# Moving a split and the end of a sum between GpSimd, VectorE and TensorE in a pipelined two-layer kernel

## What is computed

```
x = layernorm(x + attention_0(x))      # 16 heads of 8, softmax with a distance bias
x = layernorm(x + experts_0(x))        # 8 experts, top 2, silu(x W1) * (x W3) W2, and a shared one
x = layernorm(x + attention_1(x))      # each token looks at shifted copies of k and v
x = layernorm(x + experts_1(x))        # 8 linear experts, top 2
```

```
for i, off in enumerate(OFFSETS):
    if off >= N: continue
    vs = v if off == 0 else shift(v, off)
    out = out + attn[..., i:i+1] * vs
gate = sigmoid(x @ w_gate + b_gate)
return gathered * gate @ w_out + b_out
```

## Time and profile before

| | |
|---|---|
| median of 3 runs | 1559.63 us (1558.98 to 1560.1) |
| profiled execution, own time | 1561.28 us |
| its span, first to last instruction | 1559.5 us |
| TensorE busy | 1392.1 us, 89% of the span |
| VectorE busy | 1319.1 us, 85% |
| ScalarE busy | 843.3 us, 54% |
| GpSimd busy | 660.3 us, 42% |
| mean granted TensorE clock | 0.97 |
| chain that ended last | VectorE 39%, TensorE 38%, issue 10%, DMA and ScalarE 4% each |

### The profile page before, as it was taken

One profiled execution on the slowest core, in us unless ns is written; L12 is line 12 of the kernel. 1 busy time (PEld: TensorE's weight loads), 2 busy tenths in 40 slices (PEclk: granted clock), 3 DMA queues, 4 the chain that ended last, 5 costly groups with the idle time before them and its releaser, 6 DMA issues.

```text
span 1559.5 us, 34559 instructions
## 1 busy us (share of the span) xinstructions
PE 1392.1 (89%) x11872; PEld 1081.4 (69%) x11872; DVE 1319.1 (85%) x4159; ACT 843.3 (54%) x1806; POOL 660.3 (42%) x484
## 2 busy tenths in 40 slices
...
DMA packets 77931, 145.90 MB, mean 94 GB/s; under 512 B 8747, under 2 KB 64299, under 8 KB 64683
## 3 DMA queue, kind: packets, MB, share of 16 engines
...
## 4 chain that ended last, share of the span: by engine, by line
DVE 39%; PE 38%; issue 10%; DMA 4%; ACT 4%; POOL 1%; DVEq 0%; ACTq 0%; POOLq 0%; SPq 0%
DVE prod L917 8%; PE bPV L495 7%; DVE nBy L974 7%; PE bTU L479 6%; DVE mneg L1021 5%; DVE h L1031 5%; DVE nDy L955 5%; PE bS L538 4%; DMA prod<-d_w 3%; PE bTU L481 3%; PE bTU L550 2%; PE b L419 2%; PE bTU L551 2%; PE bS L541 2%; PE b L436 2%
## 5 line engine op out<-in xcount | busy, mean ns | idle before, releaser
L1085 POOL TENSOR_TENSOR prod<-prod 128x1024 f32<-128x1024 f32 (+2 forms) x160 | 290.0, 1813 | 205.7 <-DVE prod L917 198.1
L1093 POOL TENSOR_TENSOR prod<-kC,qC 128x512 f32<-128x512 f32 x256 | 322.3, 1295 | 125.7 <-ACT kC L672 125.7
L1021 DVE TENSOR_REDUCE mneg<-bS 128x2 bf16<-128x512 f32 x512 | 346.5, 693 | 32.8 <-PE bS L541 32.7
L708 ACT ACTIVATE sil<-bTU,b 128x256 f32<-128x256 f32 x288 | 136.7, 475 | 306.0 <-PE bTU L551 302.9
L698 ACT ACTIVATE P<-bTU 128x512 f32<-128x512 f32 x512 | 279.3, 603 | 11.8 <-PE bTU L481 11.4
L538 PE MATMUL bS<-stack 96*128 96x256 bf16 x1024 | 222.7, 279 | 52.3 <-DVE mneg L1021 46.1
L479 PE MATMUL bTU<-stack 97*128 97x256 bf16 x1024 | 209.8, 276 | 0.4 <-DMA stack<-mT 0.2
L541 PE MATMUL bS<-dist,identh 128*128 128x128 f16 x1024 | 198.9, 222 | 0.0
L917 DVE TENSOR_TENSOR prod<-prod,vC 128x512 f32<-128x512 f32 x256 | 185.0, 776 | 15.1 <-DMA prod<-d_w 15.1
L481 PE MATMUL bTU<-dist,identh 128*128 128x128 f16 x1024 | 192.0, 221 | 0.0
L550 PE MATMUL bTU<-x1T,w 128*128 128x256 f32 x576 | 175.9, 387 | 6.0 <-DVE h L1031 6.0
...
## 6 DMA issues: line engine op xcount, KB each, us to landing
...
```

Of the source, the lines that this page charges most:

```text
L1021: v.tensor_reduce(mneg[:, :, k], bS[k % 2][:].rearrange("p (a b) -> p a b", a=TT), op=ALU.max, axis=AX.X, negate=True).then_inc(dveS.done( ...
L1085: tt_(pv[e % 2][:, to:to + rows_, :], pv[e % 2][:, to:to + rows_, :], pv[e % 2][:, frm:frm + rows_, :], ALU.add).then_inc(poolSum.done("ad ...
L1093: tt_(prod[e % 2][:, 2 * p:2 * p + 2, :], shifted(kC, p), qC[:].unsqueeze(1).to_broadcast([128, 2, T]), ALU.mult).then_inc(poolC1.done("pr ...
```

## The change

Three things are changed.

First, GpSimd stops its sum over the 16 rows at four: C2.add.3 and C2.add.4 are gone. A new step on TensorE, C2.sm, adds the four rows with four fp32 matmuls against the identity into a bank of the bTU round (now 34 steps instead of 33), and C2.gt reads this bank. Second, A1.rest and A1.lo are done by GpSimd, and its wait for the constants moves to the pass in which A3 starts. Third, the order of the steps is new on all engines.

```
     "pool": """
-        A3.xbo C2.xb C1.prod.0 C1.prod.1 C1.prod.2 C1.prod.3 C1.prod.4 C1.prod.5 C1.prod.6 C1.prod.7 C2.add.0
-        C2.add.1 C2.add.2 C2.add.3 C2.add.4""",
+        A1.rest A1.lo C1.prod.0 C1.prod.1 C1.prod.2 C1.prod.3 C1.prod.4 C1.prod.5 C2.add.0 C1.prod.6 C1.prod.7
+        C2.add.1 C2.add.2 A3.xbo C2.xb""",
     "sp": """
-        A3.x Cs.dw A1.part.0 Cs.wb A1.part.1 C2.wb X.xT A1.part.2 A1.rows.0 A1.rows.1 A1.rows.2 M.m D2.out""",
+        A1.part.0 X.xT A1.part.1 Cs.dw Cs.wb C2.wb A3.x A1.part.2 A1.rows.0 A1.rows.1 A1.rows.2 M.m D2.out""",
...
+                    if what == "C2.sm" and (e := r["C2"]) is not None:
+                        take(turn_bank("sm", 0), ("C2", dveC2, "gt", 0), t)
+                        o = bTU[turn_bank("sm", 0)]
+                        pe.wait_ge(poolSum.sem, poolSum.count(e, "add", 2))
+                        for x in range(4):
+                            i = mm(o[:, 0:T], ident[:], pv[e % 2][:, x, :], start=(x == 0), stop=(x == 3))
+                        i.then_inc(peC2.done("sm"), 1)
...
-                        dve.wait_ge(poolSum.sem, poolSum.count(e, "add", 4))
+                        dve.wait_ge(peC2.sem, peC2.count(e, "sm"))
                         dve.wait_ge(actV.sem, actV.count(e, "g"))
                         dve.wait_ge(peC2.sem, peC2.count(e - 1, "out"))
-                        v.scalar_tensor_tensor(gat[:], tg[e % 2][:], 1.0, pv[e % 2][:, 0, :], ALU.add,
+                        v.scalar_tensor_tensor(gat[:], tg[e % 2][:], 1.0, bTU[turn_bank("sm", 0)][:, 0:T], ALU.add,
...
+                    if what == "A1.rest" and (e := r["A1"]) is not None:
+                        pool.wait_ge(actA1.sem, actA1.count(e, "hi", 1))
+                        tt_(rest[:], qk[:], parts[:, :, 0, :], ALU.subtract).then_inc(poolA1.done("rest"), 1)
+                    if what == "A1.lo" and (e := r["A1"]) is not None:
+                        pool.wait_ge(st_part[2], dma_count(e - 1))
+                        pool.wait_ge(actMid.sem, actMid.count(e, "mid"))
+                        tt_(parts[:, :, 2, :], rest[:], parts[:, :, 1, :], ALU.subtract).then_inc(poolA1.done("lo"), 1)
...
-                        to, frm, rows_ = ((0, 4, 4), (8, 12, 4), (0, 8, 4), (0, 2, 2), (0, 1, 1))[n]
+                        to, frm, rows_ = ((0, 4, 4), (8, 12, 4), (0, 8, 4))[n]
```

More of the change, by code:

```diff
@@ L49 @@
     "pe": """
[L50 to L54, removed]
+        A1.qk A1.v S.s.0 A2.ST.0 S.s.1 Cs.scT A2.ST.1 A2.ST.2 A2.ST.3 S.s.2 A2.ST.4 A2.ST.5 A2.ST.6 A2.PV.0 A2.ST.7
@@ L55 @@
+        A2.ST.8 S.s.3 A2.ST.9 A2.PV.1 B.xT A2.ST.10 S.s.4 D.xT A2.ST.11 Cs.wT S.s.5 B.lg S.s.6 D.lg C1.xT A2.ST.12
+        A2.ST.13 C1.qk A2.ST.14 A2.PV.2 A2.ST.15 S.s.7 S.s.8 B.cT D.y.0 B.ab.0 A2.PV.3 S.s.9 D.y.1 B.ab.1 S.s.10
+        A3.pT B.ab.2 B.ab.3 C1.vg B.ab.4 S.s.11 S.s.12 D.y.2 B.y.0 B.ab.5 B.ab.6 B.ab.7 S.s.13 C1.sc A3.aT B.y.1
+        B.ab.8 S.s.14 S.s.15 D.y.3 A3.out B.y.2 B.y.3 M.mT C2.sm B.z C2.out""",
     "act": """
-        A1.qk A2.exp.0 A2.exp.1 A2.exp.2 A2.exp.3 A2.exp.4 A2.exp.5 A3n.nm A2.exp.6 C2n.nm B.xT Cs.exp D.xT A2.exp.7
@@ L57 @@
-        A2.exp.8 B2.nm A2.exp.9 A1.mid Cs.wT A2.exp.10 C1.xT G.ge A2.exp.11 A2.exp.12 C1.qk A2.exp.13 A2.exp.14 B.cT
-        A2.exp.15 D2.nm B.ab.0 B.ab.1 A3.cp B.ab.2 C1.vg B.ab.3 B.ab.4 B.ab.5 A3.aT C1.sc B.ab.6 B.ab.7 B.ab.8 M.mT""",
+        A1.qk A2.exp.0 A2.exp.1 A2.exp.2 A2.exp.3 A2.exp.4 Cs.exp A2.exp.5 A2.exp.6 A2.exp.7 A2.exp.8 A3n.nm C2n.nm
+        B.xT A1.mid B2.nm D.xT Cs.wT A2.exp.9 A2.exp.10 C1.xT A2.exp.11 A2.exp.12 G.ge D2.nm C1.qk A2.exp.13
+        A2.exp.14 A2.exp.15 B.cT B.ab.0 A3.cp B.ab.1 B.ab.2 B.ab.3 C1.vg B.ab.4 B.ab.5 B.ab.6 B.ab.7 A3.aT B.ab.8
@@ L59 @@
+        C1.sc M.mT""",
     "dve": """
[L60 to L63, removed]
@@ L64 @@
-        B.acc.2 C2.gt B.acc.3 C2.res""",
+        B2.res A1.v S.max.0 D2.mom Cs.mx N.root.0 N.root.1 S.max.1 N.root.2 N.root.3 S.max.2 Cs.sum S.max.3 S.max.4
+        S.max.5 S.max.6 G.rank G.weigh S.max.7 S.max.8 D.acc.0 S.max.9 B.wu.0 D.acc.1 S.max.10 B.wu.1 C2.pv.0
+        C2.pv.1 C2.pv.2 C2.pv.3 B.wu.2 A3.rec B.wu.3 B.wu.4 S.max.11 D.acc.2 B.acc.0 A3.num B.wu.5 C2.pv.4 C2.pv.5
+        C2.pv.6 C2.pv.7 B.wu.6 S.max.12 S.max.13 B.wu.7 B.acc.1 B.wu.8 S.max.14 S.max.15 D.acc.3 B.acc.2 A3.res
+        C2.gt B.acc.3 C2.res""",
@@ L224, in network @@
         actG = steps("actG", "ge")
-        dveA1, dveS = steps("dveA1", "rest v lo"), steps("dveS", "max*16")
+        dveA1, poolA1, dveS = steps("dveA1", "v"), steps("poolA1", "rest lo"), steps("dveS", "max*16")
         dveA3 = steps("dveA3", "rec num*2 " + LN)
@@ L657, in one @@
                         act.wait_ge(st_part[1], dma_count(e - 1))
[L658 removed]
+                        act.wait_ge(poolA1.sem, poolA1.count(e, "rest"))
                         nc.scalar.copy(parts[:, :, 1, :], rest[:]).then_inc(actMid.done("mid"), 1)
@@ L893, in one @@
                 for what, n in ORDER["dve"]:
-                    if what == "A1.rest" and (e := r["A1"]) is not None:
-                        dve.wait_ge(actA1.sem, actA1.count(e, "hi", 1))
-                        v.tensor_tensor(rest[:], qk[:], parts[:, :, 0, :], ALU.subtract).then_inc(dveA1.done("rest"), 1)
                     if what == "A1.v" and (e := r["A1"]) is not None:
```

19 lines of the change are left out of this document (7 added, 12 removed).

## The result

The changed kernel takes 1551.49 us (median of 5 runs, 1548.16 to 1552.75) against 1559.63 before: ratio 0.9944, 95% interval 0.9933 to 0.9955. It is faster by 0.56%; I had predicted 1577 us, slower by 1.1%, and had given "faster" two chances in ten. The time lies inside the range, the sign is wrong. The profiled execution, on which the readings rest, took 1548.16 us (span 1546.4), against 1561.28 (span 1559.5) before: 13.1 us less in the pair of profiled executions, 8.1 between the medians (the profiled execution after is the fastest of its five runs).

A forecast was written before the change was run, and what follows sets the result against it. TensorE alone bounds: 43.18 us own work, 1.32 wait at the head and 0.45 small waits make 44.95 us a pass, 0.67 more. 27 passes add 18 us, start and drain 0: 1579 profiled, 1577 median; range 1545 to 1600.

The forecast's parts named there:

- TensorE's own work: TensorE's time in a pass without waits: 41.35 us before, plus 1.83 for C2.sm and a switch, 43.18 us.
- drain and start: Last passes without score work, and program start: -1 us and +1 us, sum 0, between -7 and +7.
- the fixed head: A2.ST.3 starts 4.78 us after A1.qk, held by ScalarE's table load and exp.0; TensorE waits 1.32 us; chance 0.48.
- wait of VectorE for xout: Sign in the changed kernel's trace: nDy was not to wait for xout.
- The small waits: TensorE waits at A2.ST.6, B.xT, D.xT and B.lg, together 0.45 us a pass.
- Edits costed at nothing: Two subtractions, A1.rest and A1.lo, moved from VectorE to GpSimd: no cost, except 1 us at program start.
- the two adds off GpSimd: Adds of 1.27 and 0.73 us removed from GpSimd: worth nothing in a full pass, as C2.gt does not wait there.
- The port between VectorE and GpSimd: VectorE's products beside GpSimd's: charged nothing; by the skill's lockout rule up to 0.8 us more a pass.
- The early Cs.mx: Cs.mx before the root in the drain: gives its chain to wb 1.5 to 2 us in three passes.
- (b): All TensorE waits go or part of its counted work was waiting: 43.18 us a pass, 1530, half 1545; chance 0.20.
- (d): Small waits and extra switch vanish, only A2.ST.3's wait stays: 44.40 us a pass, drain -3, 1560; chance 0.14.
- (c): C2.add.2 to C2.out uncovered by B.z, or B.acc.0 holds B.ab.7: 0.5 to 1.5 us a pass, 1590 to 1617; chance 0.18.

The follow-up runs named there:

- e12: Changed kernel with D.y.3 moved between S.s.14 and S.s.15 on TensorE, one more change between bf16 and fp32 matmuls; 1552.14 us.
- e3: Changed kernel with A1.rest and A1.lo back on VectorE; 1551.35 us.
- e4: Kernel before with only A1.rest and A1.lo moved to GpSimd; 1559.05 us.
- e2: Changed kernel without C2.sm, all five adds on GpSimd, the new order and the moved subtractions kept; 1571.54 us.
- e6: Changed kernel without C2.sm, five adds on GpSimd, A3.xbo and C2.xb ahead of C2.add.1, C2.gt ahead of A3.res on VectorE; 1557.03 us.
- e1: Kernel before with only C2.sm added on TensorE and three adds instead of five on GpSimd; 1596.59 us.
- e5: Changed kernel without C2.sm, five adds on GpSimd, A3.xbo and C2.xb moved ahead of C2.add.1; 1545.51 us.
- e7: Changed kernel with one matmul in C2.sm instead of four, rows 1 to 3 left out of the sum; 1524.20 us.
- e15: Changed kernel with Cs.mx behind N.root and Cs.exp behind exp.6 only in passes behind the last with S steps; 1555.42 us.

## Why the prediction was wrong

The bound was named rightly; two terms of the sum were mis-sized. TensorE's own work was put at 43.18 us a pass and measured 42.76, and drain and start were put at nothing and measured -11.3 us in the profiled pair. The first term alone takes the forecast from slower to no change: a pass of 44.33 us is nearly the 44.28 of before. It is the second that makes the kernel faster, and that gain was not foretold.

**TensorE alone as the bound, with the fixed head: right.** 81% of the chain, 4.78 us from A1.qk to A2.ST.3, 1.27 us of waits in it against 1.32. No wait of VectorE for xout, VectorE busy for 39.2 us, C2.sm 1.83 with its change of kind: all as foretold.

**TensorE's own work: mis-sized.** I had 43.18 us. Waits in the changed pass are 1.27 at the head and about 0.3 behind it, so the own work is 44.33 - 1.57 = 42.76. C2.sm is as summed; the rest fell from 41.35 to 40.93, by moving alone. About 0.3 of it lies in the gaps at changes of kind. Their number is 16 in each direction in both orders, but B.y.0, which stood directly behind S.s.15 and carried 0.14 us, now follows D.y.2, D.xT carries 0.06 instead of 0.11, and the 0.10 us that the first matmul of B.y.3 carried behind M.mT now falls on C2.sm, within its 1.83. I took such gaps as fixed; e12 shows them as 0.07 us and movable. Some 0.1 us is not accounted for.

**The small waits: nearly right.** 0.45 forecast, 0.3 found: B.xT and B.lg wait as laid out, A2.ST.6 only 0.10, D.xT not at all. With the own work as found, the pass is 44.33 and not 44.95: 0.62 x 27 = 17 us of the 31 by which the sum (1579) missed the profiled execution; the odd passes are 3 more.

**Edits costed at nothing: right for the subtractions** (e3, e4). **Wrong for the two adds off GpSimd, "worth nothing" in a full pass.** I judged them by the old order, where C2.gt didn't wait for GpSimd. In the new order A3.xbo stands behind the adds, and with all five there the pass is 44.75 at least and the total 20 us longer (e2). Of a step that is taken off a queue, what stands behind it on that queue in the new order counts too.

**The port between VectorE and GpSimd: charged nothing, rightly.** GpSimd's prod.5 ends 0.3 us before C2.pv.0 starts, and C2.pv.0 took 0.68 to 0.69 us in each of the 27 passes. So the 0.8 us a pass of the rule cited there was not put to the test in the changed kernel; e6 did so (last section).

**Drain and start: -1 and +1 forecast, -8.5 and -2.8 found**, the other 11 us. Of the three passes for which I charged C2.sm at half clock (3.5 us) only the last had it (3.75 us; the one before it 1.96), and in e1 the whole sum costs the drain 6.7 us, in the new order nothing that shows against the two adds that it replaces (216.9 against 217.6 in e5). Its matmuls are not free there: with three of the four left out the drain is 212.1 (e7). The early Cs.mx is worth up to 5 us, as I had put it (1.5 to 2 in three passes), but about half of that comes by another way, the wait at A2.PV.1 (e15). What was missing is the wait of 2.26 us at B.xT with the halved clock behind it. I read the earlier trace rows from late in the drain, where TensorE idles anyway, and took no rows of its first pass, where it is busy for 39 of 44 us and the order counts as in a full pass.

At the start, the first interval between two S.max.0 fell from 19.2 us to 16.7. It was 16.9 in e4 (subtractions moved alone) and 17.4 in e3 (subtractions back), and stayed 19.2 in e1. I had charged 1 us where some 2 were won. The subtractions alone win them, and the rest of the change wins them without the subtractions, so the two don't add up. The interval varies: in e15, which is the changed kernel there, it was 17.3.

**The rivals.** None came as written. (b) named the right cause, "part of what I count as its work", for too large an effect (43.2 us, or 43.7 with half of it); (d) had the right pass within 0.07 us and left the drain at -3. (c) didn't occur. My sum stood on a difference of 44.95 and 44.28, two numbers of which the first was made of five parts with 0.1 to 0.4 us of play each: the chance of 0.7 for slower was more than that carries.
